# Attention output scaling moved from VectorE to ScalarE, behind the next block's first two exponentials

## The reference

```python
xn  = layernorm(x)                                  # no affine part
q   = (xn @ Wq.T).reshape(b, t, 8, 256)             # 8 heads of 256
kv  = xn @ Wkv_down.T                               # 64 wide
k   = (kv @ Wk_up.T).reshape(b, t, 8, 256)
v   = (kv @ Wv_up.T).reshape(b, t, 8, 256)
att = softmax(q @ k.T * 256**-0.5)                  # no mask, full 4096 x 4096
out = (att @ v).reshape(b, t, 2048) @ Wo.T
# feed forward with 8-bit activations and ternary weights
ffn = bitlinear(silu(bitlinear(xn, w_gate)) * bitlinear(xn, w_up), w_down)
y   = x + out + ffn
```

## Time and profile before

| | us |
|---|---|
| median of the runs shown | 5639.95 |
| the three runs shown | 5639.95, 5759.88, 5421.95 |
| the profiled execution, its time | 5422.45 |
| its span on the slowest core (core 5) | 5420.9 |
| spans of the 8 cores | 5405.3 to 5420.9 |
| granted TensorE clock, mean over the span, by core | 0.866 to 0.882 |
| PE busy, DVE busy, ACT busy (core 5) | 4171.9, 2192.4, 2049.7 |

### The profile page before, as it was taken

One profiled execution on the slowest core, in us unless ns is written; L12 is line 12 of the kernel. 1 busy time (PEld: TensorE's weight loads), 2 busy tenths in 40 slices (PEclk: granted clock), 3 DMA queues, 4 the chain that ended last, 5 costly groups with the idle time before them and its releaser, 6 DMA issues.

```text
span 5420.9 us, 91414 instructions; the slowest of 8 cores (5405.3 to 5420.9 us)
## 1 busy us (share of the span) xinstructions
PE 4171.9 (77%) x24244; PEld 2312.9 (43%) x24244; DVE 2192.4 (40%) x3073; ACT 2049.7 (38%) x3331; POOL 664.0 (12%) x613
## 2 busy tenths in 40 slices
PE   1223389797997979979799795688888888099999
PEld 1112156364553645636456363344443443044444
DVE  5536622223122231222322221599988999111111
ACT  3323456363553635536355363233333333000000
POOL 2110100000000000000000000233333333000000
PEclk7555599898997989979899797898998989599999
DMA  5664411011110111101111212111111111355443
GB/s 134 145 156 132 126 36 46 26 44 36 34 44 26 44 36 34 44 25 46 36 34 44 81 51 63 51 32 40 32 38 40 32 38 30 75 159 134 121 133 109
DMA packets 535677, 350.51 MB, mean 65 GB/s; under 512 B 441920, under 2 KB 486976, under 8 KB 535168
## 3 DMA queue, kind: packets, MB, share of 16 engines
q1 hardware_dynamic: 472016, 159.44, 12.3%
q0 software_dynamic: 45648, 143.28, 9.8%
q10 hardware_dynamic: 17504, 41.95, 2.1%
HBM read 244.61 MB, written 109.05 MB: 65 GB/s over the span
## 4 chain that ended last, share of the span: by engine, by line
PE 57%; DVE 23%; DMA 8%; issue 7%; ACT 2%; SPq 1%; DVEq 1%; POOLq 0%; POOL 0%; ACTq 0%
PE psF L753 17%; PE psF L742 15%; PE psF L1044 8%; DMA arC<-x 4%; PE psF L391 4%; PE psF L922 4%; PE psF L1030 3%; DVE rsc L472 3%; PE psF L928 3%; DVE rsc L469 3%; DVE arB L475 3%; DVE arB L766 2%; DVE t L463 2%; DVE rsc L466 2%; DVE smf L946 2%
## 5 line engine op out<-in xcount | busy, mean ns | idle before, releaser
L747 ACT ACTIVATE arB<-psF 128x512 bf16<-128x512 f32 x2048 | 1210.6, 597 | 779.8 <-PE psF L742 554.8
L753 PE MATMUL psF<-arB 128*128 128x257 bf16 x8192 | 1255.9, 274 | 68.1 <-DVE arB L766 63.0
L742 PE MATMUL psF<-arB 128*128 128x512 bf16 x4096 | 1210.0, 383 | 17.4 <-DVE arB L437 17.4
L753 PEld LDWEIGHTS psF<-arB 128*128 128x128 bf16 x8192 | 771.7, 98 | 500.4 <-issue 143.4
L928 PE MATMUL psF<-arB 128*128 128x512 bf16 x2048 | 498.8, 387 | 69.9 <-DMA arB<-wuT_d 69.9
L922 PE MATMUL psF<-arA,arB 128*128 128x512 bf16 x2048 | 536.2, 409 | 13.2 <-DMA arB<-xnqT_d 13.2
L942 POOL TENSOR_TENSOR arC<-arC 128x512 f32<-128x512 f32 x256 | 425.6, 1662 | 835.1 <-ACT arC L939 835.1
L1044 PE MATMUL psF<-arB,arA 128*128 128x512 bf16 x2048 | 451.9, 381 | 68.1 <-DMA arB<-wdT_d 68.1
L762 DVE RECIPROCAL smf<-psF 128x1 f32<-128x1 f32 x256 | 43.0, 168 | 1129.7 <-PE psF L753 1108.0
L934 ACT ACTIVATE arC<-psF,smf 128x512 f32<-128x512 f32 x256 | 175.9, 687 | 728.1 <-PE psF L928 596.0
L742 PEld LDWEIGHTS psF<-arB 128*128 128x128 bf16 x4096 | 402.5, 98 | 102.4 <-issue 28.5
(11 more groups left out here) (128 smaller groups left out, 3508.8 us busy)
## 6 DMA issues: line engine op xcount, KB each, us to landing
arC<-Wg POOLq DMA_DIRECT2D x64, 512.0 KB, 5.6
arC<-Wu POOLq DMA_DIRECT2D x64, 512.0 KB, 5.8
arC<-Wd POOLq DMA_DIRECT2D x64, 512.0 KB, 6.2
hqT_d<-p1b SPq DMA_DIRECT2D x32, 1024.0 KB, 6.2
arA<-hqT_d SPq DMA_DIRECT2D x32, 1024.0 KB, 8.8
arC<-x SPq DMA_DIRECT2D x32, 512.0 KB, 9.0
aoT_d<-arB SPq DMA_DIRECT2D x64, 256.0 KB, 2.1
arC<-x ACTq DMA_DIRECT2D x32, 512.0 KB, 8.6
```

The costliest lines, as they stand in the source:

```text
L742: p.add("tensor", lambda e, bi=bi, c=c, g=g, d2=d2: e.matmul(bank(g), kT[:, d2 * T + c * 128: d2 * T + (c + 1) * 128], qT[:, d2 * T + bi * ...
L747: p.add("scalar", lambda e, g=g, c=c: e.activation(pT[c % 3][:, :], bank(g), AF.Exp, bias=0.0, scale=ISCL), reads=[b_bank[g]], writes=[b_p ...
L753: p.add("tensor", lambda e, c=c, sub=sub: e.matmul(pv_ps(sub, 0, 257), pT[c % 3][:, sub * 128:(sub + 1) * 128], vA[:, c * 257:(c + 1) * 25 ...
```

## The change

The four scalings of each block leave DVE and become ACT activations (function Identity, with the reciprocal as the per-partition scale). The four reciprocals stay on DVE. For blocks 0 to 6 of a head the scalings are added after the scores of chunk 1 of the next block, so that in ACT's order they stand behind that block's exponentials of chunks 0 and 1 and ahead of that of chunk 2. For block 7 they follow the reciprocals at once.

```diff
-            def finalize_evac():
+            def finalize_recips():
                 for sub in range(4):
                     p.add("vector", lambda e, sub=sub: e.reciprocal(
                         repl[:, sub:sub + 1], pv_ps(sub, 256, 257)),
                         reads=[b_bank[3 + sub]], writes=[b_repl])
+
+            def finalize_atto(bi):
                 for sub in range(4):
-                    p.add("vector", lambda e, sub=sub: e.tensor_scalar(
+                    p.add("scalar", lambda e, sub=sub: e.activation(
                         att_o[:, sub * 256:(sub + 1) * 256], pv_ps(sub, 0, 256),
-                        repl[:, sub:sub + 1], None, op0=ALU.mult),
+                        AF.Identity, scale=repl[:, sub:sub + 1]),
                         reads=[b_bank[3 + sub], b_repl], writes=[b_atto],
-                        extra=(b_wkvT.handover() if h == 0 and sub == 0 else ()))
+                        extra=(b_wkvT.handover()
+                               if h == 0 and bi == 0 and sub == 0 else ()))
...
                 for c in range(NTC):
                     emit_qk(bi, c)
+                    if c == 1 and bi >= 1:
+                        finalize_atto(bi - 1)
                     if c >= 4:
...
                 emit_pv(NTC - 2)
                 emit_pv(NTC - 1)
-                finalize_evac()
+                finalize_recips()
+                if bi == 7:
+                    finalize_atto(7)
```

## The result

The changed kernel is slower by 1%: the ratio to the kernel before is 1.0101, 95% interval 1.0060 to 1.0142. Put on the profiled execution of before, 5422.45 us, that is 5477 us; the forecast of 5466 us stood for 1.008. The medians of ten runs each are 5613.09 us (5471.79 to 5874.35) after and 5641.02 us (5421.95 to 5776.08) before; they rank the other way because most runs were disturbed, some cores having a lower clock for a long time, and the ratio is taken from the undisturbed ones, three of ten on either side (5471.79 to 5496.84 us against 5421.95 to 5432.20).

A forecast was written before the change was run, and what follows sets the result against it. PE was taken to set the pace inside blocks, with scalings costing time only at boundaries. 5422.45 us + 31.6 (pauses) - 17.4 (head ends) + 29.7 (clock) gave 5466 us; range 5415 to 5700.

The forecast's parts named there:

- Duration and pace: At block boundaries: a scaling on ACT takes 0.476 us against 0.484 on DVE, each waiting for the last, stepping 0.57 us.
- Start: At a block boundary, ACT's first scaling starts 1.67 us after the first score matmul, 0.64 us later than on DVE.
- Pause: PE's fourth matmul starts 0.6 us later at 48 block boundaries, 0.35 at eight first ones: +31.6 us.
- Head ends: At eight head ends DVE's weight work, freed of the scalings, starts 2.17 us earlier, shortening the chain: -17.4 us.
- The clock: After longer boundary pauses PE's clock falls at 19 of 56, one already before, costing 1.65 us each: +29.7 us.
- The sum: Whole kernel: 5422.45 + 31.6 - 17.4 + 29.7 = 5466 us, 0.8% over the profiled execution; chance 0.45.
- What 5466 stands for: Whole kernel: the time belongs to executions like the profiled 5422.45 us; in the same ratio the median would be 5685.
- Clock holds: Rival, at block boundaries: the pause grows but PE's clock does not fall; 5437 us, chance 0.24.
- Overlap: Rival, at block boundaries: ACT's scalings overlap, stepping 0.37 us, and PE loses nothing; 5405 us, chance 0.08 with other gains.
- Falls at every boundary: Rival: PE's clock falls after all 56 block boundaries, costing 91 us; 5528 us in all, chance 0.20.
- second table load: Rival, on ACT: Identity and Exp share no table, so two loads at each of 64 blocks add 164 us; chance 0.03.
- mean clock over the span: Sign, over the profiled span: a mean PE clock no lower than before would show the forecast wrong.

The follow-up runs named there:

- run without the self-wait: The changed kernel with a separate buffer for each quarter of the scaled output, so ACT's four scalings do not wait for one another; 5393.98 us, 0.996 of the fastest before.
- run behind chunk 0: The changed kernel with the scalings one exponential earlier in ACT's order, after that of chunk 0 instead of chunk 1; 0.9977 of the kernel before.
- filled run: The changed kernel with chunk 2's score matmuls issued four times in blocks 1 to 7, six useless matmuls more per boundary; 5431.89 us, 1.003 of the fastest before.
- run behind chunk 2: The changed kernel with the scalings one exponential later in ACT's order, after that of chunk 2 instead of chunk 1; 5533.77 us, 1.023 of the fastest before.
- the one with the head ends alone: The changed kernel with only block 7 of each head scaled on ACT, blocks 0 to 6 back on DVE; 0.9963 of the kernel before.

## Why the prediction was right or wrong

- **Duration and pace.** 0.476 us a scaling, measured 0.475; a step of 0.57, measured 0.57. The rule of the Trainium skill (ScalarE: Activation LUTs, Rules for kernel authors) that a multiplication belongs on VectorE was not borne out by this trace, with float32 in PSUM as the source: 475 ns on ACT, 484 on DVE. The run without the self-wait shows that the step was the wait and not ACT's own pace.
- **Start.** +1.67, measured +1.67. The run behind chunk 0 moved it, and the pause with it by the 0.49 us between two exponentials.
- **Pause.** +31.6 us over 56 boundaries; measured +29.
- **Head ends.** -17.4 us over eight; measured -19 over seven (2.7 us each instead of 2.17), and shown alone at 0.9963. At the one shown, 2.32 of the 2.55 us are gained by the time of the copy: the weight work had been held by 2.34 us, from the end of the reciprocals, and not by the 2.17 that the prediction read.
- **The clock.** This is the term of the sum that was mis-sized: "I take a third, 19". The clock fell at 27 or 28 boundaries, half of them, and cost 43 us by the stage's balance and 44 to 46 by the filled pause, against 29.7. The price of one fall, 1.65 us, was right (1.67 between the two blocks shown). The share was wrong, and it was a guess: the prediction put the eight first boundaries of a head, with 3.7 to 3.9 us, into one group. The trace of before, read on all eight cores, held a sharper row. There the clock fell at 5 of the 16 pauses of 3.89 or 3.90 us and at none of the 432 up to 3.81. A third was the share at 3.9 us already; at 4.1 us it was half.
- **The sum.** +0.8% predicted, +1.0% measured; parts +29, -19 and +43 against +31.6, -17.4 and +29.7. The change moved the time the way the sum said, and 1.008 lies within the measured interval. That the total came so near is in part luck: the clock's term was 13 us too small, and by the prediction's own bounds it could have been anything from 10 to 91 us.
- **What 5466 stands for.** This step failed too. The sum was added to 5422.45 us, the profiled execution, 3.9% under the median of the runs, and given as the time. Against the median of before, 5641.02 us, 5466 reads as a gain of 3%, and the change was a loss of 1%. The prediction names the figure that belongs to the median, 5685; the median after was 5613.09, because medians of such runs differ by more than the change is worth. Only the ratio can be held against the result.
- **The rivals.** "Clock holds" fell with 27 falls; what it described is the filled run, 5431.89 us against its 5437. "Overlap" fell for the changed kernel, and came true, also for the clock, when the shared buffer went (5393.98 us against its 5405). "Falls at every boundary" is the run behind chunk 2, at 1.023. No second table load was seen.
- **A sign that could not tell.** A mean clock over the span no lower than before was named as a sign of being wrong. It was 0.866 to 0.869 on cores 0 to 3, against 0.866 to 0.882 on the eight cores before: 28 falls are too little for the mean over the span. Over attention alone it was 0.91, against 0.92 (core 2, core 5).

## What to carry to other kernels

Before an operation is moved to a less busy engine, read from a timeline where in that engine's order it will stand, and what it waits for there: here both engines needed the same time for it, and the new place cost 0.6 us a boundary before any effect on the clock. A buffer that four independent operations share as a whole makes an engine wait for its own semaphore; splitting the bookkeeping was worth 1.5%, more than any choice of engine in these runs. And a pause of the matmul engine has two prices, its own length and the clock afterwards: look at the granted clock behind each pause, and test it with work that changes nothing.

## What the runs showed of the hardware that was not expected

- Six useless 128x512 matmuls in a pause made the kernel faster: 2631.8 against 2671.5 us of attention, with 0 falls against 27 or 28.
- In unfilled pauses, all with the same six score matmuls and four short ones, the share that falls grew from none to nearly all between 3.8 and 4.6 us. In the kernel before, the one with the head ends alone and the one behind chunk 0, eight cores each, the clock fell at none of the 1304 pauses up to 3.81 us and at 18 of the 40 of 3.89 or 3.90. In the changed kernel it fell at 110 of 224 (4 cores, mostly 4.10 us), and behind chunk 2 at 446 of 448 (4.6 us).
- Boundaries of the same length differ in their fate. In the changed kernel those into a block with an odd number fell at 22 to 24 of 32, those into one with an even number at 3 to 5 of 24, nearly all with the same pause of 4.10 us. Why was not settled, and the two runs with the scalings behind chunk 2 (54 to 56 falls unfilled, 0 or 1 filled, with a stretch of poor work of the same length) show that length alone is not the rule.
- An operation that waits for the one before it on the same engine stepped by 0.57 us instead of 0.365 on ACT (0.475 long), and by 0.59 instead of 0.39 on DVE (0.484 long).
- The filled run keeps some 5 us of loss that neither pauses nor falls explain (16 us of attention over before, of which the pauses give 29 and the head ends take 18). Some 3.5 us of it lie in the q, k and v work of the next heads (483.7 us in seven heads against 480.2, medians of eight cores), which no edit touches; the cause stays open.
